# A one-core tower kernel: tokens in natural order, and the last pair's expert stage as one unit per batch

## The reference

```python
h = tok(ids)                       # Fourier features of 4 id tables -> relu(f @ W1 + b1) @ W2 + b2, LayerNorm, + 0.1 * residual
h = h + attn(layernorm(h))         # 8 heads, scores = q k^T * scale, softmax, ctx; ctx is reshaped to (H*KD, s) before Wo
h = h + ffn(layernorm(h))          # 6 experts, top 2

def attn(x, Wq, Wk, Wv, Wo):
    q = einsum('bsc,oc->bso', x, Wq).reshape(b, s, H, KD).transpose(0, 2, 1, 3)
    k = einsum('bsc,oc->bos', x, Wk)
    v = einsum('bsc,oc->bos', x, Wv).reshape(b, s, KD)
    p = softmax(einsum('bhsd,bdt->bhst', q, k) * scale)
    ctx = einsum('bhst,btd->bhsd', p, v).transpose(0, 2, 1, 3).reshape(b, H * KD, s)
    return einsum('bcp,oc->bop', ctx, Wo).transpose(0, 2, 1)

def ffn(x):
    top_w, top_i = top_k(softmax(relu(x @ rw1 + rb1) @ rw2 + rb2), 2)
    y = relu(relu(x @ e1 + b1) @ e2 + b2) @ e3 + b3      # for each expert
    return sum over the two chosen experts of y * softmax(top_w)
```

## Time and profile before

| | before |
|---|---|
| median of 3 runs | 669.76 us (667.29 to 671.34) |
| the profiled execution's own time | 672.91 us |
| its span, first to last instruction | 671.1 us |
| TensorE busy | 644.7 us, 96% |
| VectorE / ScalarE / GpSimd busy | 539.1 / 476.0 / 279.7 us |
| granted TensorE clock over the span | 0.983 |

### The profile page before, as it was taken

The page is one execution under the profiler, slowest core; times in us unless marked ns, Lnnn a source line. Parts: engine busy times, 40 slices in busy tenths (PEclk is TensorE's granted clock), DMA queues, the critical chain, the costliest instruction groups (busy, mean ns, idle before and its releaser), DMA issues.

```text
span 671.1 us, 26756 instructions
## 1 busy us (share of the span) xinstructions
PE 644.7 (96%) x11632; PEld 360.9 (54%) x11632; DVE 539.1 (80%) x1068; ACT 476.0 (71%) x1193; POOL 279.7 (42%) x354
## 2 busy tenths in 40 slices
PE   7699999999999999999999999999999999999974
PEld 6345555555555466555655465555655555555653
DVE  4588678988788887989788887989889897977555
ACT  2388885887668866887668867697758875888331
POOL 1134112704763175622945156630947037311372
PEclk9799999999999999999999999999999999999978
DMA  4000000000000000000000000000000000000001
GB/s 173 1 2 2 2 2 3 2 2 2 19 4 2 2 3 19 3 2 2 4 19 2 2 3 20 2 2 3 3 19 2 2 3 19 2 2 2 4 2 32
DMA packets 9428, 6.66 MB, mean 10 GB/s; under 512 B 8672, under 2 KB 8672, under 8 KB 9184
## 3 DMA queue, kind: packets, MB, share of 16 engines
q1 hardware_dynamic: 9312, 4.97, 2.6%
HBM read 2.87 MB, written 2.10 MB: 7 GB/s over the span
## 4 chain that ended last, share of the span: by engine, by line
PE 90%; DVE 5%; ACT 2%; issue 1%; POOL 1%; DMA 1%; ACTq 0%; SPq 0%; DVEq 0%; POOLq 0%
PE s_bank L470 33%; PE s_bank L438 32%; PE s_bank L560 5%; PE s_bank L450 4%; PE s_bank L662 3%; PE s_bank L627 3%; PE s_bank L638 3%; PE s_bank L480 2%; ACT p L742 1%; PE s_bank L491 1%; PE s_bank L533 1%; PE s_bank L507 1%; PE s_bank L602 1%; PE s_bank L518 1%; POOL st L1177 1%
## 5 line engine op out<-in xcount | busy, mean ns | idle before, releaser
L742 ACT ACTIVATE p<-s_bank,nmax 128x512 f32<-128x512 f32 x512 | 347.3, 690 | 122.2 <-DVE nmax L868 121.7
L868 DVE TENSOR_REDUCE nmax<-s_bank 128x1 f32<-128x512 f32 x512 | 323.3, 681 | 36.2 <-PE s_bank L438 35.7
L438 PE MATMUL s_bank<-kf,g 64*64 64x512 f32 x2048 | 255.6, 597 | 1.1 <-DVE g L949 0.8
L470 PE MATMUL s_bank<-p,woz 64*64 64x256 f32 x4096 | 245.6, 378 | 1.8 <-ACT g L748 1.4
L470 PEld LDWEIGHTS s_bank<-p,woz 64*64 64x64 f32 x4096 | 153.6, 133 | 116.5 <-issue 37.6
L295 POOL TENSOR_TENSOR woz<-cst,rz 128x256 f32<-128x256 f32 x126 | 77.3, 634 | 246.9 <-DVE rz L874 246.9
L438 PEld LDWEIGHTS s_bank<-kf,g 64*64 64x64 f32 x2048 | 73.2, 134 | 91.2 <-issue 47.9
L742 ACT ACTIVATION_READ_ACCUMULATOR p<-s_bank,nmax 128x1 f32 x512 | 105.4, 206 | 0.0
L880 DVE STREAM_TRANSPOSE m<-s_bank 128x512 f32<-128x512 f32 x64 | 45.7, 714 | 24.5 <-PE s_bank L470 24.5
L1177 POOL TENSOR_TENSOR st<-st,power 128x8 f32<-128x8 f32 x24 | 39.5, 1644 | 37.7 <-DVE st L895 37.7
L304 POOL TENSOR_TENSOR y<-y,gt 128x768 f32<-128x768 f32 x28 | 41.3, 1475 | 17.6 <-DVE y L1094 17.6
(11 more groups left out here) (118 smaller groups left out, 504.4 us busy)
## 6 DMA issues: line engine op xcount, KB each, us to landing
tower_out<-o SPq DMA_DIRECT2D x16, 128.0 KB, 2.6
cst<-consts SPq DMA_DIRECT2D x1, 1070.0 KB, 8.5
e2t<-ids SPq DMA_DIRECT2D x1, 768.0 KB, 5.8
cst<-consts SPq DMA_DIRECT2D x1, 416.0 KB, 6.3
cst<-consts SPq DMA_DIRECT2D x1, 288.0 KB, 3.7
e2t<-ids SPq DMA_DIRECT2D x1, 256.0 KB, 3.5
cst<-consts SPq DMA_DIRECT2D x1, 3.0 KB, 1.8
```

The costliest lines, as they stand in the source:

```text
L438: last = pe.matmul(double[half(q), 512 * r:512 * r + 512], g[half(r), a // 2 % 2, a % 2, first:first + 64], kf[half(r), par, a // 4, :], s ...
L470: last = pe.matmul(bank("PV", i, a)[half(q), 512 * hh:512 * hh + 256], woz[half(r), kept, 2 * mm + hh, :], keys[:, q, :, :], start=(part = ...
L742: nc.scalar.activation(p[:, 8 * kept + c % 8, :], bank("S", i, c - r)[:, 512 * r:512 * r + 512], ACT.Exp, bias=nmax[:, c % 16:c % 16 + 1], ...
L868: nc.vector.tensor_reduce(nmax[:, c % 16:c % 16 + 1], bank("S", i, c - r)[:, 512 * r:512 * r + 512], AX.X, ALU.max, negate=True).then_inc( ...
```

## The change

**Natural order.** A tile is now 128 consecutive tokens of one batch: tiles 0 to 3 are the pair's first batch, 4 to 7 its second. The ids are laid out accordingly on the host, the key copies interleave by tile, and a store writes four tiles of 128 partitions. In FIN the two partition halves of a tile are now two heads of the same batch, so a matmul takes every second head of one batch: 128 matmuls of 128 columns instead of 64 of 256.

**Units.** The expert stage is written for a unit: a pair, or some tiles of it. Pair 7 has two units, tiles 0 to 3 and tiles 4 to 7, with semaphores and a table (`L[0]`, `L[1]`) each; the second one's FIN is in two parts (tiles 4 to 6, tile 7). Each of their steps works on 4 tiles instead of 8. All tables have new numbers (of `F` one line is shown).

```diff
-    ids: t.reshape(n, PAIRS, 2, HEADS, KD).transpose(0, 1, 3, 2, 4).reshape(n, PAIRS, QUARTERS, QT)...
+    ids: t.reshape(n, PAIRS, QUARTERS, QT)...
 F = {
-    "FIN": 12, "LN": 13, "SQ": 15, "LN2": 16, "T": 23, "T_ACT": 23, "R": 28, "R_ACT": 25, "L": 33,
+    "FIN": (12,), "LN": 13, "SQ": 16, "LN2": 20, "T": 29, "T_ACT": 29, "R": 31, "R_ACT": 31, "L": 34,
...
+LAST_PARTS = ((0, 4), (4, 7, 8))
+L = ({"FIN": (49,), ...}, {"FIN": (71, 71), ...},)
+UNITS = tuple((i, (0, 8), F) for i in range(PAIRS - 2)) + ((PAIRS - 2, (0, 8), Z),) + tuple(
+    (PAIRS - 1, parts, f) for parts, f in zip(LAST_PARTS, L))
...
-            def value_products(i, par, *heads):
-                for n in range(8):
-                    for g4 in range(4):
-                        q, s2 = g4 // 2, g4 % 2
-                        for b2, first, end in heads:
-                            last = pe.matmul(
-                                bank("FIN", i, s2)[half(b2), 512 * q + 32 * first:512 * q + 32 * end],
-                                v[quarter(g4), par, b2, n, :], m[quarter(g4), b2, first:end, n, :],
-                                start=(n == 0), stop=(n == 7), skip_group_check=True)
+            def value_products(u, t0, t1):
+                par = u.i % 2
+                for b2 in range(2):
+                    lo, hi = max(t0, 4 * b2), min(t1, 4 * b2 + 4)
+                    if lo >= hi:
+                        continue
+                    for n in range(8):
+                        for g4 in range(4):
+                            q, s2 = g4 // 2, g4 % 2
+                            for c in range(2):
+                                last = pe.matmul(
+                                    bank("FIN", u.u, s2)[half(c), 512 * q + 32 * lo:512 * q + 32 * hi],
+                                    v[quarter(g4), par, b2, n, :],
+                                    m[quarter(g4), b2, 2 * (lo - 4 * b2) + c:2 * (hi - 4 * b2):2, n, :],
+                                    start=(n == 0), stop=(n == 7), skip_group_check=True)
...
-            def fin_part(n):
-                ...
-                value_products(i, par, *(((0, 0, 8), (1, 0, 4)), ((1, 4, 6),), ((1, 6, 8),))[n]).then_inc(fin_parts, 1)
+                for n, (lo, hi) in enumerate(zip(u.parts, u.parts[1:])):
+                    if slot == f["FIN"][n]:
+                        ...
+                        pe.wait_ge(mtd, HH * u.i + hi)
+                        value_products(u, lo, hi).then_inc(u.fin_ps, 1)
...
-            def outputs(i, j, src):
-                dve.wait_ge(y_pool, 4 * W_SUM * i + (W_LAST if j == 2 else 0))
+            def outputs(u, n, j, src):
+                first = units[PAIRS - 1].pool0
+                dve.wait_ge(y_pool, first + (W_LAST if j == 2 else 0))
...
-            for n in range(PAIRS):
-                store(n, n == PAIRS - 1)
+            for u in units[:PAIRS - 1]:
+                sp.wait_ge(y_pool, u.pool0 + 4 * W_SUM)
+                for b2 in range(2):
+                    store(u.i, b2)
+            for b2 in range(2):
+                sp.wait_ge(y_pool, units[PAIRS - 1].pool0 + (b2 + 1) * W_LAST)
+                sp.wait_ge(y_dve, 2 * (b2 + 1))
+                store(PAIRS - 1, b2)
```

More of the change, by code:

```diff
@@ L135, in ring_order @@
                 prep(i + 1, slot)
-            if i:
-                ffn(i - 1, slot, F if i + 1 < PAIRS else Z)
-            if i + 1 == PAIRS and slot == L["FIN0"]:
-                order.extend([("FIN", i, 0), ("FIN", i, 1)])
+            for u, when in active(i, slot):
+                ffn(u, when)
     for slot in range(SLOTS):
@@ L143, in ring_order @@
             order.append(("PV", *found))
-        ffn(PAIRS - 2, slot + SLOTS, Z)
-        ffn(PAIRS - 1, slot, L)
+        for u, when in active(PAIRS, slot):
+            ffn(u, when)
     return order
@@ L163, in read_at @@
         return SLOTS * (i - 1) + slot + 1
-    f = F if i + 2 < PAIRS else Z if i + 2 == PAIRS else L
+    pair, parts, f = UNITS[i]
     if name in ("FIN", "XT", "R", "L"):
@@ L179, in ring_places, with last, tiles, cols @@
     return place
+@dataclass
+class Norm:
+    xc: object
+    sq: object
+    st: object
+    sums: object
+    steps: object
+    squared: object
+    n: int
+    count: int
+    tiles: slice
+@dataclass
+class Unit:
+    u: int
+    i: int
+    parts: tuple
+    f: dict
+    n: int
+    pool0: int
+    dve0: int
+    norm: Norm
+    fin_ps: object
+    hatt_sb: object
+    x2t_ps: object
+    xt_sb: object
+    rh_ps: object
+    rh_sb: object
+    l_ps: object
+    gate: object
+    gate_act: object
+    gated: object
+    e1_ps: object
+    e1_sb: object
+    e2_ps: object
+    e2_sb: object
+    y_ps: object
+    y_sb: object
+    @property
+    def last(self):
+        return self.i == PAIRS - 1
+    @property
+    def tiles(self):
+        return slice(self.parts[0], self.parts[-1])
+    @property
+    def cols(self):
+        return slice(64 * self.parts[0], 64 * self.parts[-1])
+    @property
+    def js(self):
+        return range(self.parts[0] // 2, self.parts[-1] // 2)
 def tower(nc, ids, consts, out):
@@ L465, in pv @@
                         pe.wait_ge(wozd, 2 * (HH * i + a) + mm // 2 + 1)
+                    if not part and mm == 0:
+                        free("PV", i, a)
                     for r in range(2):
@@ L689, in body @@
                         prep(i + 1, 1 - par, slot)
-                    if prev:
-                        ffn(i - 1, 1 - par, slot, F if nxt else Z)
-                        ffn_out(i - 1, slot, F if nxt else Z)
-                    if not nxt and slot == L["FIN0"]:
-                        fin_part(0)
+                    for u, when in active(i, slot):
+                        ffn(units[u], when)
+                        ffn_out(units[u], when)
             def warm(count, bank):
@@ L829, in body @@
                         prep(i + 1, 1 - par, slot)
-                    if prev:
-                        ffn(i - 1, slot, F if nxt else Z)
+                    for u, when in active(i, slot):
+                        ffn(units[u], when)
             def sines(n):
@@ L1067, in ffn @@
-                    dve.wait_ge(hatt_sb, 4 * i + 4)
-                    mean(2, i, after)
-                    if f is L:
-                        centred(2, after, i)
+                                                    bank("FIN", u.u, s2)[:, 512 * q + 32 * t0:512 * q + 32 * t1].rearrange(
+                                                        "q (t c) -> q t c", c=32), ALU.add).then_inc(u.hatt_sb, 1)
+                    if u.last:
+                        dve.wait_ge(before_last.norm.steps, 3 * before_last.n + 3)
```

653 lines of the change are left out of this document (351 added, 302 removed), and 14 rows, old and new, of tables (F, L, Z).

## The result

The changed kernel takes 691.4 us (median of 4 runs, 689.05 to 697.63), the kernel before beside it 669.4 (667.29 to 671.34): ratio 1.033, 95% interval 1.028 to 1.039, so +22 us (+19 to +26). A second series (e4) gives 1.034 (1.029 to 1.039). The forecast was 681 with 666 to 689: the sign was right, the size too small by 10 us, and the time lies above the range.

What follows compares the result with a forecast made beforehand. TensorE was taken to bound the middle, a chain of waits the 38.6 us tail. Narrow matmuls +2.9, late blocks +13.3, last pair -2.3 and tail -2.2 gave +11.7 on 669.8: 681 us, range 666 to 689.

Steps and rivals of the forecast that it cites:

- T0: End of the last PV, at 632.49 us in the kernel before; forecast to move by +13.9 us.
- the tail: From the end of the last PV to the end of the span: 36.4 us against 38.6, so -2.2.
- The late blocks: In each narrow FIN, TensorE stops for instruction blocks arriving late: 1.9 us each, +13.3 us for seven.
- Narrow matmuls: FIN of pairs 0 to 6 as 256 half-wide records at 15.9 ns: 0.42 us more each, +2.9 us.
- The new slot numbers: Tables of the middle pairs: the new numbers cost nothing as long as TensorE stays full.
- Pair 7: Last pair before the last PV's end: Y0 and first FIN part leave, first unit's FIN (2.03 us) comes: -2.3 us.
- GpSimd's three sums: Pair 6's sums in the tail, behind the power step: 4.04 us each, ending 23.9 us after the last PV.
- the second unit's last gate steps: VectorE's gate work in the tail, done while GpSimd sums and pair 6 is stored; given no time of its own.
- The base: The +11.7 us, worked out on the profiled execution, was put on the median of the runs, 669.8 us.
- A: Rival: instruction blocks arrive in time, so no FIN stops: -3.1 us, 666.7 us; chance 0.22.
- B: Rival: each FIN pays one stop of 0.99 us, like the one seen: +5.3 us, 675 us; chance 0.15.
- C: Rival: block latency 3.5 us instead of 3.7, and power step 0.8 us less with its width: 677 us; chance 0.10.

Runs made afterwards that it cites:

- e4: The changed kernel measured again, nothing altered; ratio to the kernel before 1.034 (1.029 to 1.039).
- e1: Kernel before with FIN of pairs 0 to 6 as 256 matmuls of 128 columns, a bank's two column halves by turns; ratio to before 1.025.
- e16: Kernel before with the narrow FIN in one piece, heads 0 to 3 first, then heads 4 to 7; ratio to before 1.018.
- e15: Changed kernel with 32 small matmuls (128 instructions, half a block) more at TensorE's start, moving the block borders; ratio to before 1.038.
- e7: Changed kernel with VectorE's fifth gate step moved from slot 39 to 41 and ScalarE's second from 39 to 42; ratio to before 1.034.
- e13: Changed kernel with the tables A, P and F of the kernel before; ratio to before 1.047.
- e18: Changed kernel with 32 small matmuls (128 instructions) in front of the FIN of the last pair's first unit; ratio to before 1.038.
- e17: Changed kernel without 7 of the 22 VectorE gate steps in each of the last pair's two units; ratio to before 1.033.
- e9: Kernel before with narrow FIN of pairs 0 to 5 in quarters over slots 9 to 12, pair 6's in one piece; ratio to before 1.025.
- e8: Changed kernel with ScalarE's exponential of the first unit's gate moved from slot 97 to 91; ratio to before 1.034.

## Why the prediction was wrong in size and right in sign

**By stages.** Between the two traces, and without before's 3 us of slow clock at the start, the six pairs are +17.1 (forecast 13.9, six sevenths of 16.2), pair 6's FIN to T0 +1.3 (forecast 0), the tail +1.4 (forecast -2.2). So the terms miss by 3.2, 1.3 and 3.6 us. The start is some 0.6 shorter than in e1 and e16. The rest of the 10 us, some 3, lies between the two profiled executions and the medians.

**The late blocks: the mechanism right, the sum right in part by luck.** Forecast +13.3 for seven FINs; the stops of the profiled run sum to 13.2 (1.34, 1.76, 1.82 and 1.06, 0.49 and 2.19, 1.46, 1.62, 1.49). Every one stands at a 256-instruction border, and e15 moved them with it. The split among blocks was not as I had it. I gave the first border 0.4 us, the second 1.4, the third 0.1. A border whose block began ahead of FIN costs nothing in six of seven FINs (0.49 once); one whose block lay wholly in FIN costs 1.3 to 2.2 each time; the one behind it costs 1.06 once. Too much at the first border and too little at the second (1.7 on the mean) cancel. The packet of a stop starts 2.3 to 2.9 us before the stream goes on, and the next one 1.0 to 1.7 after; added for each stop of the changed kernel and e15 that is 3.3 to 4.1 for a block, against the 3.7 that I took. The Trainium skill's rule ("Runtime: NRT & Kernel Launch", section "Instruction fetch mechanics"), that the fetch is hidden, does not agree with 19 such stops in the traces of the changed kernel and e15 alone.

**Narrow matmuls: somewhat too dear.** I took 15.9 ns a record and +2.9. The pace within FIN is 14.5 ns, but from FIN's first record to the next line's it takes 3.8 to 3.95 us without its stops, where it took 3.64: +0.24 each, +1.7 for seven, within my bounds. Both terms together are 14.9 instead of 16.2. e16, which has them and nothing else, measures +12 (10 to 14); by its own trace they are 13.0.

**The new slot numbers: the first step that failed.** "The new slot numbers of the middle cost nothing as long as TensorE stays full." TensorE did not stay full: on line 538 it waits 3.8 us in the middle for VectorE's eviction, and the six pairs are 3.9 us longer than narrow matmuls (1.4) and stops (11.8) make them: 17.1 against 13.2. Against e16 the changed kernel needs 5.3 us more for them (475.6 and 470.3). That wait and 1.3 us more of issue (eight stops, where e16 has six) are 5.1 of it. But this names only where the time stands. e7 shows that the wait is handed on when it is taken away, and with the old tables (e13) only 1.7 of the 5.3 go. Of e13's other 3.6 over e16, 1.0 is a wait of PV for ScalarE and 1.4 more of issue; the rest is small pieces. That the natural order makes them is not shown; no run varied it alone.

**Pair 7: right, but the cut between the stages hid it.** FIN of the first unit takes 2.10 us as forecast (2.03). Counted by the starts of their records, FIN and Y steps are 2.3 us less than in e16 between pair 6's FIN and T0, yet the stage is only 0.4 shorter (68.8 against 69.2). The changed kernel has one query product more in it (24 records instead of 16, 0.8 us), which in e16 stands ahead of pair 6's FIN; waits for ScalarE are 0.5, PV is 0.4 longer. So the six pairs' 5.3 is rather 6.1.

**The tail: the second step that failed, a stop put at nothing.** Forecast 36.4, measured 40.0. I had one stop behind T0, in FIN (1.5; 1.32 on the chain), and none for what stands behind FIN. The FIN of the last unit is followed by 8 transposes (16 records) without a wide matmul between them, so a second block ran dry there: 1.87 us on the chain, and Y1 of pair 6 with GpSimd's sums stands behind it. VectorE evicts Y1 ahead of the second unit's reduction, so the power step starts at T0 + 11.5 (forecast 10.1); with the border elsewhere it starts at 9.3 (e15) and 9.0 (e18), and the tails are 37.3 and 36.5. Nor do GpSimd's three sums stand in one piece, as I had them: the third waits 2.1 us for VectorE's eviction and ends at T0 + 26.7 (forecast 23.9). The power step is 1.02 us at its width of 4, where I took 1.65:
```profile
658.68 1.02 POOL L1308 TENSOR_TENSOR st<-st,power 128x4 f32<-128x4 f32 x1 [5.00 <-DVE st L1007]
...
669.86 1.47 POOL L389 TENSOR_TENSOR y<-y,gt 128x768 f32<-128x768 f32 x1 [2.13 <-DVE y L1224]
```
VectorE's gate work in the tail, which I had priced as "the second unit's last gate steps", is in truth 50 instructions and 11.8 us, where before had 23 and 4.9; but e17 shows that it is covered but for 1 us at most, so it was a wrong count almost without a price. Of before's 38.6 about 1 us may again be the clock (0.84 from 640 to 660 us): e1, e9 and e16, whose tails are the same program, have 37.3 to 37.9.

**The base: +16 in the traces, +22 in the medians.** I set the difference on the median, which was right, but did not see that the trace of before held some 3 us of slow clock at its start. And the stops seem to have a second price that the first profiled run does not show. In some executions the clock falls behind a long stop. e17: the window with a stop of 2.2 at 427.9 us, the one behind it, and one more behind a stop of 1.9 at 510 us:
```profile
427.00:431.00 4.00, 2.08 (x124) 1.66 (x113) 0.88 (x3) 1.84 (x5) 0.00 (x0) 1.00 0.02 6
431.00:434.00 3.00, 3.00 (x32) 1.95 (x36) 2.25 (x6) 0.00 (x0) 0.60 (x1) 0.52 0.03 5
...
513.00:517.00 4.00, 4.00 (x41) 2.39 (x44) 2.27 (x6) 0.00 (x0) 1.04 (x1) 0.57 0.00 0
```
PV runs there at 1.2 GHz, half pace, for 3 to 4 us, which costs 1.5 to 2. e8 shows the same at 353 and 514 us behind stops of 1.9 and 2.2. Both have 480.8 to 480.9 us for their six pairs, the profiled run 475.6; e7 and e18, without such a fall in the middle, have 476.4 and 475.3. That this is also why the changed kernel's runs spread over 8.6 us and those of before over 4 is likely and not shown: the longest, 697.63, has the lowest granted clock, 0.978, the others have 0.985 to 0.992, and it has no trace.

**Rivals.** A (blocks arrive in time) fell at once. B (0.99 a FIN) named 675, C 677. The 0.05 for a time above 689 was too small: I had bounded each known term and left no room for a cost in the tables, though I had noted that they were laid anew, nor for a stop behind the last FIN.

## What to carry to other kernels

Halving a matmul's width doubles the instructions for the same columns. Where 256 of them run dry in less than the 3.3 to 4.1 us that a block takes here (an estimate from the packets' starts), expect TensorE to stop at the border, whatever the other engines do; count instructions per microsecond for every dense stretch, also the one behind the stretch that you changed. Read the granted clock of the profiled run by stage before it is used as a base: 3 us of it were not the kernel's. And in a program whose engines are all laid out by slot, price any new table by the nearest measured pair, not at zero.

## What was not expected of the hardware

- The stop as such is 1.3 to 2.2 us at a border behind a wholly dense block, in 14.5 ns records; at 18 to 19 ns (e1) 0.5 to 1.4.
- The pace of 14.5 ns belongs to records that go around the corners of the array. The 64 of e18 with the same 32x64 weights, all in one corner, took 65 ns each (4.2 us).
- A stop of 1.9 to 2.2 us can be followed by 3 to 4 us at half clock (0.50 to 0.52 in e8 and e17), in one execution and not in another: the stop of 2.19 at 347 us in the profiled run had a clock of 1.00 behind it.
- Two column halves of one PSUM bank, accumulated by turns, gave other sums (e1) than one half after the other (e16). The Trainium skill's page "PSUM — Partial Sum Buffer", section "The four PSUM rules", says why: the first matmul of a group clears the written marks of the whole bank over the partitions it writes, so the other half's next product overwrites instead of adding. The two runs agree with it.
- Small VectorE steps beside a GpSimd step took up to four times as long: line 1135, 128x24, 0.83 and 0.57 us in the tail of the changed kernel, where its neighbours take 0.19. Both end within 0.1 us of the end of the GpSimd step that runs beside them, and so do e15's two, 0.27 and 0.56 us. No run varied it, so that it waits for that step is a reading.
```profile
665.48 0.83 DVE gt L1135
666.33 0.19 DVE gs L1138
```
The GpSimd step beside the first:
```profile
665.26 0.99 POOL L397 TENSOR_TENSOR ys<-y 128x384 f32<-128x384 f32 x1
```
